# A fused RWKV, retention and two-expert-layer kernel: y kept in slot order in the first expert layer, x scattered with its choices, expert stages unrolled

## The reference

```python
x = x + _L0_attn_a_ref(_layernorm(x), W_rvk, W_out, time_decay, time_first)   # RWKV time mixing
x = x + _L0_ffn_ref(_layernorm(x), ...)                                       # experts
x = x + _L0_attn_b_ref(_layernorm(x), ...)                                    # retention, 16 heads
x = x + _L0_ffn_ref(_layernorm(x), ...)                                       # experts, same weights
```

```python
logits = flat @ router_w
scores = softmax(logits)
_, topk_idx = top_k(logits + router_bias, 4)
topk_scores = take_along_axis(scores, topk_idx); topk_scores /= topk_scores.sum(-1)
g = silu(einsum('nd,edf->nef', flat, wg)); u = einsum('nd,edf->nef', flat, wu)
routed = einsum('ne,nef,efd->nd', comb, g * u, wd)
shared = ...   # silu(x @ swg) * (x @ swu) @ swd
return routed + shared
```

## Time and profile before

| | us |
|---|---|
| median of 3 runs | 1926.53 (1919.05 to 1931.41) |
| profiled execution | 1934.83 |
| its span | 1933.1 |
| time mixing, to 232 | 232 |
| first route stage, 232 to 491.6 | 260 |
| first expert stage, 491.6 to 849.15 | 358 |
| retention, 849.15 to 1262.6 | 413 |
| second route stage, 1262.6 to 1514 | 251 |
| second expert stage, 1514 to 1869.8 | 356 |
| last sum, 1869.8 to 1933.1 | 63 |

### The profile page before, as it was taken

One profiled execution on the slowest core, in us unless ns is written; L12 is line 12 of the kernel. 1 busy time (PEld: TensorE's weight loads), 2 busy tenths in 40 slices (PEclk: granted clock), 3 DMA queues, 4 the chain that ended last, 5 costly groups with the idle time before them and its releaser, 6 DMA issues. The chain is left out here.

```text
span 1933.1 us, 26797 instructions
## 1 busy us (share of the span) xinstructions
PE 1502.8 (78%) x7368; PEld 1028.5 (53%) x7369; DVE 1101.8 (57%) x2797; ACT 531.7 (28%) x1007; POOL 858.5 (44%) x860
## 2 busy tenths in 40 slices
PE   6576478998788898828898999768898788888930
PEld 3243345554666676614555555545555567666720
DVE  6666486662444544534757576667664344545538
ACT  5766421221222222203030303132221222222200
POOL 3656557564355555531020202037676155555630
PEclk9888678999888987958898979878999889779865
DMA  9600062125544543234333330052225445444229
GB/s 363 275 1 1 15 252 85 70 93 139 148 134 143 151 133 108 60 107 170 133 133 132 132 132 0 2 240 84 75 96 143 124 143 149 142 135 124 75 111 324
DMA packets 133028, 245.38 MB, mean 127 GB/s; under 512 B 24594, under 2 KB 94278, under 8 KB 132436
## 3 DMA queue, kind: packets, MB, share of 16 engines
q1 hardware_dynamic: 101684, 176.74, 28.8%
q0 software_dynamic: 30720, 67.74, 9.5%
q10 hardware_dynamic: 544, 0.00, 0.0%
HBM read 121.38 MB, written 139.74 MB: 135 GB/s over the span
## 5 line engine op out<-in xcount | busy, mean ns | idle before, releaser
L1057 POOL DMA_INDIRECT pairs_y<-arena x384 | 380.3, 990 | 364.1 <-DVE arena L1159 239.9
L816 POOL DMA_INDIRECT slots_x<-arena x256 | 268.2, 1048 | 126.0 <-issue 72.8
L1090 PE MATMUL moe_eh<-arena 128*128 128x128 f32 x1536 | 251.2, 317 | 76.6 <-DVE arena L1151 70.8
L1090 PEld LDWEIGHTS moe_eh<-arena 128*128 128x128 f32 x1536 | 229.0, 229 | 86.8 <-ACT arena L1123 84.0
L1164 DVE TENSOR_TENSOR arena<-arena,moe_eh 64x256 f32<-64x256 f32 x192 | 81.1, 423 | 321.7 <-PE moe_ey L1103 197.2
L1103 PE MATMUL moe_ey<-arena 64*128 x768 | 248.3, 450 | 1.3 <-DVE arena L1172 1.3
L1123 ACT ACTIVATE arena<-moe_ext 128x512 f32<-128x512 f32 x192 | 114.9, 598 | 251.2 <-PE moe_ext L1079 128.5
L1103 PEld LDWEIGHTS moe_ey<-arena 64*128 64x128 f32 x768 | 146.9, 212 | 45.5 <-issue 12.6
L1079 PE MATMUL moe_ext<-ident,arena 128*128 128x128 f32 x768 | 140.6, 312 | 20.3 <-DMA arena<-slots_x 13.2
L659 PE MATMUL moe_down<-arena 128*128 128x256 f32 x512 | 130.7, 412 | 23.3 <-DVE arena L937 14.8
L1079 PEld LDWEIGHTS moe_ext<-ident,arena 128*128 128x128 f32 x768 | 91.0, 155 | 92.2 <-issue 78.1
(11 more groups left out here) (222 smaller groups left out, 2194.6 us busy)
## 6 DMA issues: line engine op xcount, KB each, us to landing
slots_x<-empty_slots SPq DMA_DIRECT2D x96, 520.0 KB, 8.8
arena<-slots_x SPq DMA_DIRECT2D x192, 260.0 KB
arena<-pairs_y SPq DMA_DIRECT2D x64, 512.0 KB
arena<-w_gu SPq DMA_DIRECT2D x2, 8192.0 KB
pairs_y<-arena POOLq DMA_INDIRECT x384
residual<-x SPq DMA_DIRECT2D x8, 512.0 KB
slots_x<-arena POOLq DMA_INDIRECT x256
out<-residual SPq DMA_DIRECT2D x4, 1024.0 KB
```

Of the source, the lines that this page charges most:

```text
L816: pool.indirect_dma_start(out=slots.x, in_=tiles_of(ring, n, depth)[:, j, :], in_offset=None, out_offset=bass.IndirectOffsetOnAxis(ap=slot ...
L1057: pool.indirect_dma_start(out=slots.y, in_=ytile[:, n % YRING, j, :], in_offset=None, bounds_check=slots.pairs - 1, oob_is_err=False, out_ ...
L1090: last = pe.matmul(h_ps[place % 2][:, j * P:(j + 1) * P], weights[:, place % 2, j, h, :], xt[:, place % 2, (j * KH + h) * P:(j * KH + h + ...
```

## The change

**First expert layer.** y is stored in slot order by SP, one transfer a pair (`slots_y`), and no pair numbers travel with x. `slot` moves from the arena of the stage to `k.slot`, and in retention Pool gathers each tile's four choices by it (`Choices.gather`, four indirect DMAs a tile, 128 in all) where SP loaded before. **Second layer.** y is still scattered. A row of x carries its token's four experts and four pair numbers (`TAIL = 8`), written once, and DVE finds the pair number of a slot by comparing the experts with that of the slot tile (`find_targets`, every other pair). **Route stages.** The normalised rows of all 32 tiles stay in one buffer `xn`; there is no second copy, no `renumber`, no ring to wait for, and Pool scatters token tile by token tile. `power` goes as (0,1), (1,2), (2,6), (6,8), and DVE takes the statistics of blocks 0 to 4 ahead of `choose(0)`. Four small DVE operations in `slots_of` permute the slots so that each partition reads and writes two neighbouring rows of a pair of tiles (`(s p t)` where it was `(s t p)`), one piece of 2048 or 2112 bytes. **Expert stages.** There is no register loop: 96 steps are written out. The hidden part is 2 steps behind the transposes, the down part 4 (`HIDDEN, DOWN = 2, 4`); `weights`, `ht` are 3 deep. `wd` of both experts of a pair is first copied to `wd_pair`, one on partitions 0 to 63 and one on 64 to 127, and so are the two halves of `ht`; the two down products write two PSUM banks. In the first layer Pool copies `weights` (2 copies of 128x256 a pair) and one half of `wd_pair`, ACT the other half; in the second DVE copies `weights` and ACT both halves.

```diff
+    def gather(self, pool, t):
+        self.free(pool, t)
+        for i in range(self.K):
+            pool.indirect_dma_start(out=self.ring[:, t % self.G, i, :], in_=self.k.slots.y, out_offset=None,
+                                    in_offset=bass.IndirectOffsetOnAxis(ap=self.k.slot[:, t, i:i + 1], axis=0))\
+                .then_inc(self.sem(f"in{t % self.G}"), 16)
...
-                steps.link(dve.tensor_copy(slot[:, BLK * n:BLK * (n + 1), :].rearrange("p t i -> p (t i)"), slot_f))
+                steps.link(dve.tensor_copy(row, slot_f))
+                steps.step(dve.tensor_scalar(within, row, P - 1, None, ALU.bitwise_and))
+                steps.link(dve.tensor_scalar(odd, row, P.bit_length() - 1, 1, ALU.logical_shift_right, ALU.bitwise_and))
+                steps.link(dve.scalar_tensor_tensor(within, odd, float(1 - P), within, ALU.mult, ALU.add))
...
         def _(pe):
+            def hidden(n):
+                pe.wait_ge(sem("weights_ready"), 2 * (n + 1))
+                pe.wait_ge(sem("xt_read"), n + 1)
+                if n >= 2:
+                    pe.wait_ge(sem("ht_ready"), n - 1)
...
+            def down(n):
+                pe.wait_ge(sem("ht_ready"), n + 1)
+                for j in range(2):
+                    pe.wait_ge(sem(f"wd_ready{j}"), n + 1)
+                if n >= 2:
+                    pe.wait_ge(sem("y_kept"), n - 1)
+                for j in range(2):
+                    rows = slice(j * F, (j + 1) * F)
+                    last = pe.matmul(y_ps[n % 2][:, j, 0:D], ht[rows, n % 3, j * P:(j + 1) * P],
+                                     wd_pair[rows, n % 3, :], start=True, stop=True)
...
+            for s in range(NP + DOWN):
+                if s < NP:
+                    transposes(s)
+                if HIDDEN <= s < NP + HIDDEN:
+                    hidden(s - HIDDEN)
+                if s >= DOWN:
+                    down(s - DOWN)
...
+            def gate_up(n):
+                if n % RING == 0:
+                    load_experts(mybir.EngineType.Pool, held, n)
+                if n >= 3:
+                    pool.wait_ge(sem("h_full"), n - 2)
+                for j in range(2):
+                    copy_weights(pool, held[n][j], n, j).then_inc(sem("weights_ready"), 1)
```

More of the change, by code:

```diff
@@ L1019, in pair_of, with load_experts @@
-        def pair_of(g, r, s, back):
-            if s is not None and not 0 <= s - back < NP:
-                return None
-            turn = g if r >= back else g - 1
-            place = (r - back) % RING
-            return RING * turn + place, turn, place
-        def load_experts(engine, held, g, pairs):
-            row = expert_row[0:1, bass.ds(2 * (RING * g + pairs[0]), 2 * len(pairs))]
+        def load_experts(engine, held, first):
+            row = expert_row[0:1, 2 * first:2 * (first + RING)]
@@ new lines, in stage_down @@
+            def stage_down(n):
+                if n == 0:
+                    act.wait_ge(k.wd_in, 16 * WD_LOADS * turn)
+                if n % RING == 0:
+                    load_experts(mybir.EngineType.Activation, held, n)
+                if n >= 3:
+                    act.wait_ge(sem("y_full"), n - 2)
+                for j in range(0 if scatters else 1, 2):
+                    act.activation(wd_pair[j * F:(j + 1) * F, n % 3, :], down_of(held[n][j]), ACT.Copy)\
+                        .then_inc(sem(f"wd_ready{j}"), 1)
```

588 lines of the change are left out of this document (288 added, 300 removed).

## The result

The changed kernel is slower. It took 1954.55 us, the median of 4 runs (1948.92 to 1959.97), against 1925.2 for the kernel before (4 runs, 1919.05 to 1931.41): a ratio of 1.0152, with a 95% interval of 1.0108 to 1.0196, so 1.5% and clear of 1. The forecast was 1782. Timed again later (run c2_after_again) the ratio was 1.0232 (1.0148 to 1.0315).

The account below looks back on a forecast made before the run. PE's signals were taken to arrive late while Pool issues more than two indirect transfers in a row. Terms -113 - 40 + 31 - 22 = -144 from 1934.8 gave 1790.8, less 8.3 to the median: 1782 us, range 1710 to 1885.

Parts of the forecast that it names:

- What bounds the kernel: Expert stages: PE's signals reach others late during Pool's scatter runs, 3.4 us a pair instead of 2.54.
- Everything after the second gather of each run: Retention's upper bound for held signals: 34 us a batch for three batches plus 15 at the start, 115.
- A route stage speaks against making it a law: Route stage of the kernel before: a Silu started amid twelve scatters; only the next was 4.76 us late.
- The two route stages: Both route stages: copies, renumbering, ring waits and PE's wait before block 3 go; -11 each, -22 (-28 to -10).
- the power of block 3: Route stages: PE stands 10.0 us before block 3's transposes since power(3, 5) stood behind sixteen scatters.
- Retention: Retention: 128 Pool gathers replace 32 loads, delaying the start and holding some signals; +31 (+16 to +131).
- the signal effect: Retention: PE's signals held during gather runs, between nothing and 115 us; 15 taken.
- The second expert stage: Second layer's expert stage, still scattering: 3.02 us a pair, between 2.58 and 3.45; -40 (-81 to 0).
- The first expert stage: First layer's expert stage, no scatters: PE sets the pace at 2.2 us a pair; -113 (-139 to -93).
- Gathers hold PE in retention: Rival, retention: gathers hold PE's signals, +100, 1882 us in all; chance 0.14.
- The loop is the cause: Rival, expert stages: the loop or double descriptors cause late signals, which all go; -210, 1716 us; chance 0.18.
- Slower: Rival, first expert stage: Pool's copies cost 1.4 us each, 4.5 a pair, +221, 2003 us; chance 0.05; slower overall 0.04.

Follow-up runs that it names:

- e12: Changed kernel, Pool waiting for landing after each 8 route scatters and each tile's 4 gathers, second-layer y stored by SP, last sum gathering; 1800.1 us, 0.9331 of before.
- e6: Changed kernel with one small Pool operation after every 4 or 2 route scatters, each tile's 4 gathers and every second pair in second expert stage; 1918.9 us, 0.9911 of before.
- e16: Changed kernel with breaks after each 8 route scatters: six small Pool operations in the first stage, a wait for landing in the second; 1851.4 us.
- e10: Changed kernel without any indirect DMA, the kernel of e3 again, on a chip where before takes 1926.4 us; 1654.7 us.
- e14: Changed kernel with Pool waiting for landing after each 8 route scatters and each tile's 4 gathers; 1821.3 us, 0.944 of before.
- e4: Kernel before with both expert stages written out, no register loop, on the chip where before took 1786.7 us; 1744.2 us.
- e3: Changed kernel without any indirect DMA, on the chip where before took 1786.7 us; 1654.6 us.
- e8: Changed kernel with second-layer y stored by SP, weights copied by Pool, last sum gathering, and landing waits after each 4 route scatters; 1866.1 us.
- e7: Kernel before with first-layer y stored in slot order by SP, no scatters there, loops kept on engines other than SP; 1861.7 us.
- e13: Kernel before with first-layer y stored in slot order by SP and both expert stages written out, no register loop; 1823.2 us.

## Why the prediction was wrong

- **What bounds the kernel** was read rightly in its two regimes: PE's signals are late during Pool's runs. It was then not applied to the route stages. ("Everything after the second gather of each run" overstates it: 4 gathers or 8 scatters in a row with breaks cost nothing in e12.) The step that failed is "A route stage speaks against making it a law: there Silu starts at 448.68 in the middle of twelve scatters". One Silu is one signal. I did not ask how long the runs would be after the change: they are 32 and 16 long. Before, the 16 scatters of a block were broken up, as in these POOL rows of the kernel before:

```profile
314.64 1.67 POOL L816 DMA_INDIRECT slots_x<-arena  x1 [3.60 <-ACT arena L705]
...
320.09 0.21 POOL L809 COPY arena<-arena 128x4 int32<-128x4 int32 x1
320.57 0.98 POOL L816 DMA_INDIRECT slots_x<-arena  x1 [0.28 <-issue]
```

In nine of the 16 blocks of the two route stages Pool waits 3.5 to 7.4 us, 40.3 in all, after the first four scatters, until ACT has put the pair numbers behind the second copy of the rows; `renumber` adds breaks of mostly 0.5 to 0.7 us, and waits for landing only twice (3.2 and 3.5 us). The second copy was listed as a saving, and the wait for it had been a break. No run put one kind of break back alone, but e6's 0.4 us did little and e16's 1.3 us was enough.
- **The two route stages**, "-11 a stage, -22 (from -28 to -10)": measured +34.8 and +48.3. Without late signals the stages do take 249 to 250 and 247 to 249 (e10, e12, e14, e16), 7 to 11 less than before on such a chip, but not for my reasons: before's own route code takes 246 and 249 where nothing is late (e4), so the copies, the ring waits and the power of block 3 cost nothing (PE's stand before block 3's transposes is there in e4 too, 6.73 us), and the 7 to 11 are signals held in before too. Late signals add 46 to 63 in the changed kernel. The two terms miss by 105 us, of the 164 between the forecast sum (-144) and the measured one (+20).
- **Retention**, +31: measured +65. The start, +16, is right (41 us instead of 24.5); "the signal effect ... I take 15" should have been 46. Both ends of the range, nothing and 115, were stated; I took one near the low end, "as in the route stage", which rests on the same Silu.
- **The second expert stage**, -40: measured +14.5. "A third weight buffer and a deeper lag let Pool run longer, but by my reading longer runs also hold PE's signals longer" was the mechanism; that the middle of the bounds should follow from it was no step at all. The cycle is 8 scatters (10.1 us) and 4.6 of stop. What ends the run at eight isn't shown: four y buffers hold as many, but DVE waits there for ACT's Silu and ACT for PE, not for a buffer. Without scatters the stage takes 235 us (e3, e10), and with the weight copies on Pool as well 213 to 214 (e8, e12).
- **The first expert stage**, -113: measured -143. The mechanism is right; the pair took 2.12 and not 2.2 us (the down products 0.63, between 0.55 and 0.92), which is 8 us, and the 10 for late signals were not there. The other 12 are the ends of the stage, which the sum took as unchanged but for 3 us more: they were 20 us (12 before the first scatter, 8 after the last), and 11 remain. The runs divide it, on chips where signals are late: 358 with loop and scatters, 291 without scatters, 262 without loop (e7, e13), 214 with the rest of the edits, that is deeper lags, down products in two row groups and weight copies on Pool. The Trainium skill's rule on mode switching ("TensorEngine Tiling (Array Packing)", Key Properties) would show at the rows at 632.02 and 632.65. There is no gap, but ends of PE rows are modelled, and 0.63 us is 0.16 more than two passes of 0.23; so the trace rules out a large cost and not a small one. Pool's copies took 398 ns (x192) and 394 ns (x96), below the 0.5 that I took.
- **The rivals.** "Gathers hold PE in retention", 0.14, happened in part: 46 us in the loops of the 115 that it was priced from. "The loop is the cause" was 0.18 as a whole; it is 29 us of a stage where nothing else is late. That fits the Trainium skill ("Runtime: NRT & Kernel Launch", Instruction fetch mechanics: a taken branch out of the two pages forces a fetch), and PE's 2.10 us with no releaser at 604.13 agrees with it, but no run here shows a fetch. "Slower" got 0.04 because I looked for it at Pool's copies, not in the stages that I had down as savings.

## What to carry to other kernels

Look at how long GpSimd will issue indirect DMAs in a row after a change, not only at how many there are: PE's signals may reach nobody until the run ends. In these route stages runs of 8 with 1.3 us of something else between them cost nothing, and in retention's chunk loops runs of 4 with a wait for landing; in the expert stages even 6 to 8 in a row held PE's signals; a break of 0.4 us after each 4 gave back 30 of some 128 us there (e6), and to scatter nothing gave back all of it. An edit that removes a wait may remove the pause on which another engine lived; and the same kernel should be timed on more than one chip before a time is explained.

## What the runs showed of the hardware

- While Pool issues indirect DMAs 0.3 us apart, PE's completion signals arrive late (14.4 us for the up product above) and come out 1.2 to 2.4 us after the run ends. How soon in a run it begins differs: the eighth scatter of the route's run held nothing, and in the expert stages six to eight were enough. Gathers do it as scatters do (46 us in retention's chunk loops, gone with breaks). Copies on Pool (288 in the first expert stage, at 2.12 us a pair) don't.
- It is so on the chips where before takes 1922 to 1935 us. On one chip, where it takes 1787 (one execution), 16 scatters in a row held nothing. Without indirect DMAs the kernel took 1654.6 and 1654.7 us on a chip of either kind. Why chips differ stays open; so does the path on which the signals wait. Open too is why retention took 406 us, not 413, in the two runs with before's expert stages unrolled (e4, e13).
- A turn of a register loop of 8 pairs cost PE 2.0 to 2.1 us of standing, and the stage 29 us for its 11 turns (e7 against e13).
- Two 64-row products of 256 columns on separate halves of the rows and in two PSUM banks took 0.63 us a pair of tiles (start to start), against 1.05 in before, where one followed the other.
